# Layer 0 attention of a two-layer kernel: probability sums on GpSimd, value matmuls in two halves between the scores, three work banks

## The chip, the cores and the metric

The kernel runs on one core of a Trainium2 chip. The metric is the device time of one execution in microseconds. PE is TensorE (matmuls; PEld is its weight loads), ACT is ScalarE, DVE is VectorE, POOL is GpSimd, SP is the queue that issues DMAs. PSUM has eight banks of 128 partitions by 512 float32; GpSimd's instructions here read and write SBUF alone.

## The reference, cut to what matters

The program is two transformer layers with several kinds of attention and feed-forward. The change touches the first attention only: two batches of 1024 tokens, hidden size 128, 16 heads of 64, 4 key/value heads, causal.

```
q = (h @ Wq.T) ... ; k, v likewise with 4 heads, each repeated 4 times
scores = einsum("bhqd,bhkd->bhqk", q, k) * 64 ** -0.5 + causal
probs  = softmax(scores)          # exp(s - max) / sum over keys
out    = einsum("bhqk,bhkd->bhqd", probs, v) ... @ Wo.T
```

## The kernel before, in words

`stage_attention64` works in 8 **groups** g, one for each key/value head and batch; a group holds 4 query heads (`REP`). A group has 12 **steps**: a step is one tile of 128 keys (`kt`) against one **chunk** of 512 queries (`qc`). Chunk 0 has key tiles 0 to 3, chunk 1 has 0 to 7. Where a key tile lies on the diagonal the step is narrower: `unit_lo` leaves 512, 384, 256 or 128 query columns in the last four tiles of a chunk. So a group has 4,608 query columns, as many as nine full steps of 512.

In step n PE computes the scores of step n, transposed (keys on partitions): for each head one fp32r matmul with 128 rows (`qA`,`kH`, line 539) and a second of 65 rows (`qB`,`kL`, line 540) that adds the small parts and the negated row maximum. Three score banks take turns. ACT writes exp of them as float32 into a probability tile (line 723); three such tiles take turns (`P64`, `RING = 3`). On diagonal tiles GpSimd zeroes one 128-column block of each head by an affine select (line 740). Two steps later (`LAG = 2`), as the last thing of its step, PE runs `values(n)`: eight float32 matmuls (line 562; the trace shows two records for each) of 32 output columns each, that four at a time fill the four column strips of the array and add probabilities times V into the banks `O[0]` and `O[1]`; then four more of the same form with a matrix of ones (line 566) that add the row sums of the probabilities into a bank of their own, `SUMS`.

Between the scores PE does **jobs** for the next group ("fills"): `proj` (line 491, the q and k projections, split by ACT at lines 695 and 698 and by DVE at lines 606 and 611 into a high and a low part), `max` (lines 501 and 507, scores of raw form whose row maximum DVE takes, line 621), `turn` (line 513, a transpose of the maxima, which four DMAs lay into `qB`), and for a finished chunk `fin` (line 519, the output projection, which DVE adds to `y`, line 633). A job writes one of two work banks in turn, and PE waits until DVE has freed the bank of the job two before it. `spread_over` assigns `proj` and `max` jobs to steps by their column width, `proj` with weight 3; `parts` hands a step's jobs out after its score matmuls, ceil(jobs / score jobs) after each until none is left. The last group has no `proj` or `max` jobs to do.

When a chunk is closed, `copy_out` takes O[0] (ACT, line 707), the sums into `S64` (DVE, line 642) and O[1] (DVE, line 643) out of PSUM; SP gathers the sums into a dense tile (line 776), DVE takes reciprocals (line 649), SP writes them to DRAM and spreads them over partitions (lines 784, 789), DVE multiplies (line 656, both inputs in SBUF), and `fin` follows. After the last chunk DVE takes the reciprocal straight from `SUMS` (line 673), PE spreads it with a selection matrix (line 582). Each engine runs its own program in the written order, with semaphores between them.

## Time and profile before

| | us |
|---|---|
| three runs | 1538.16, 1543.96, 1883.71 |
| median | 1543.96 |
| the profiled execution, first to last instruction (span) | 1535.8 |
| layer 0 attention in it, first score matmul to last sum matmul | 60.4 to 662.5 |

A window or a timeline gives times from the span's start. "Busy" of PE is modelled, since matmuls are pipelined; what a matmul costs in a dense stream is read from the distance between two starts. In a row of the timeline, brackets give the engine's idle time before the instruction and what ended it.

### The profile page before, as it was taken

To read this page: it belongs to the slowest core of one execution; us is meant where nothing else is said; L and a number is where in the kernel's file an instruction comes from. 1 tells how busy PE (TensorE), PEld (TensorE's weight loads), DVE (VectorE), ACT (ScalarE), POOL (GpSimd) and SP (SyncE) were. 2 spreads that over 40 slices of the span, in tenths; PEclk is the share of its full clock that TensorE was granted. 3 is DMA by queue.
4 is the path that set the end of the run, shared out by engine and by line. 5 is a ranking of instruction groups with operands and counts; after the bars stand their busy time and mean duration, and the time that the engine had idled before them with its cause. 6 is when DMAs were issued, how large, how long until landed. Compare 5 with 4: busy or idle time off the path is not lost. (4 is left out here: it accounts for less than half of the span.)

```text
span 1535.8 us, 21410 instructions
## 1 busy us (share of the span) xinstructions
PE 1313.7 (86%) x7772; PEld 774.5 (50%) x7772; DVE 976.1 (64%) x1750; ACT 692.4 (45%) x1319; POOL 115.2 (7%) x155
## 2 busy tenths in 40 slices
PE   4688999999999999966999996526898888789998
PEld 3344444454545454444888874413343333256886
DVE  4455464545555454146999985756777666257998
ACT  2232334342424252433666665421566556525664
POOL 0000000000000000000000000120211111020000
PEclk9698999999999999987999998855899989868998
DMA  3101111120201020104576640022222210102220
GB/s 103 40 15 34 29 34 34 33 48 15 48 19 43 15 43 15 30 0 96 130 159 146 150 92 1 1 35 90 56 55 57 47 47 20 43 21 78 76 103 28
DMA packets 51476, 81.61 MB, mean 53 GB/s; under 512 B 16749, under 2 KB 34453, under 8 KB 47445
## 3 DMA queue, kind: packets, MB, share of 16 engines
q1 hardware_dynamic: 51004, 79.40, 21.1%
q10 hardware_dynamic: 384, 1.05, 0.6%
q8 instruction: 55, 0.90, 0.3%
q14 instruction: 33, 0.26, 0.1%
HBM read 63.75 MB, written 5.68 MB: 45 GB/s over the span
## 5 line engine op out<-in xcount | busy, mean ns | idle before, releaser
L621 DVE TENSOR_REDUCE mraw<-ps 128x1 f32<-128x512 f32 (+3 forms) x304 | 192.7, 659 | 131.1 <-PE ps L507 74.0
L1329 PE MATMUL ps<-qA 128*128 128x512 f32 x960 | 252.9, 400 | 15.2 <-POOL qA L1439 10.6
L723 ACT ACTIVATE shared<-ps 128x512 f32<-128x512 f32 (+1 forms) x216 | 119.4, 567 | 263.3 <-PE ps L540 261.9
L1046 DVE TENSOR_REDUCE mraw<-ps 128x2 f32<-128x1024 f32 (+3 forms) x160 | 173.7, 1114 | 67.6 <-PE ps L954 46.1
L1329 PEld LDWEIGHTS ps<-qA 128*128 128x128 f32 x960 | 182.1, 192 | 64.2 <-POOL qA L1439 12.3
L1101 ACT ACTIVATE shared<-ps 128x512 f32<-128x512 f32 (+2 forms) x320 | 154.4, 561 | 124.7 <-PE ps L970 124.4
L539 PE MATMUL ps<-qA,kH 128*128 128x512 f32 (+3 forms) x384 | 167.8, 447 | 5.8 <-DMA qB<-mT 5.8
L501 PE MATMUL ps<-kH,qA 128*128 128x512 f32 (+3 forms) x384 | 138.8, 415 | 34.9 <-DVE qA L611 18.8
L1393 ACT CAST qA<-shared 128x512 fp32r<-128x512 f32 x160 | 99.3, 621 | 90.4 <-DVE shared L1531 88.9
L1341 PE MATMUL ps<-qA,kH 128*128 128x512 f32 x480 | 136.3, 393 | 4.1 <-DVE qA L1455 4.1
L540 PE MATMUL ps<-qB,kL 65*128 65x512 f32 (+3 forms) x384 | 132.8, 356 | 0.0
L539 PEld LDWEIGHTS ps<-qA,kH 128*128 128x128 f32 x384 | 75.3, 196 | 80.1 <-issue 61.8
L1455 DVE TENSOR_TENSOR qA<-shared,qA 128x512 fp32r<-128x512 f32 x160 | 110.0, 688 | 7.0 <-ACT qA L1393 2.0
L501 PEld LDWEIGHTS ps<-kH,qA 128*128 128x128 f32 x384 | 70.2, 198 | 83.7 <-DVE mraw L621 52.6
L1531 DVE TENSOR_TENSOR shared<-shared 128x512 f32<-128x512 f32 x156 | 106.7, 684 | 0.0
L1341 PEld LDWEIGHTS ps<-qA,kH 128*128 128x128 f32 x480 | 90.1, 189 | 25.1 <-DVE qA L1455 6.4
L562 PE MATMUL ps<-shared 128*32 128x512 f32 (+3 forms) x1024 | 100.9, 512 | 0.3 <-DVE oU L643 0.3
L723 ACT ACTIVATE rB<-ps 128x512 f32<-128x512 f32 x88 | 51.8, 598 | 107.9 <-PE ps L540 107.0
L970 PE MATMUL ps<-qA,kH 64*128 64x512 f32 (+3 forms) x288 | 79.7, 443 | 14.5 <-ACT shared L1101 7.6
L943 PE MATMUL ps<-kL,qA 64*128 64x512 f32 (+3 forms) x288 | 67.3, 452 | 25.5 <-DMA kH<-qB 16.5
L611 DVE TENSOR_TENSOR qA<-ps,qA 64x512 fp32r<-64x512 f32 x64 | 44.1, 689 | 70.6 <-ACT qA L698 70.1
L996 PE MATMUL ps<-shared,VP 128*32 128x512 f32 (+3 forms) x768 | 87.3, 530 | 0.8 <-ACT oU L1088 0.5
(247 smaller groups left out, 1747.1 us busy)
## 6 DMA issues: line engine op xcount, KB each, us to landing
shared<-comb SPq DMA_DIRECT2D x92, 256.0 KB, 4.3
qB<-qA SPq DMA_DIRECT2D x16, 512.0 KB, 4.8
rB<-a0rec_dram SPq DMA_DIRECT2D x60, 128.0 KB, 2.9
shared<-comb SPq DMA_DIRECT2D x7, 1024.0 KB, 4.4
rB<-a1rec_dram SPq DMA_DIRECT2D x28, 128.0 KB, 2.6
e0wUp<-in_w SPq DMA_DIRECT2D x48, 64.0 KB, 4.6
qA<-q_split SPq DMA_DIRECT2D x24, 128.0 KB
q_split<-qA SPq DMA_DIRECT2D x4, 512.0 KB
```

Source lines behind the costliest of these rows:

```text
L501: ins = nc.tensor.matmul(bank[:, i * width:(i + 1) * width], k.qA[par][:, h0 + i, qt * P:(qt + 1) * P], k.kH[par][:, ch * 512:ch * 512 + w ...
L539: nc.tensor.matmul(out, k.kH[par][:, keys], k.qA[par][:, h, cols], start=True, stop=False)
L540: ins = nc.tensor.matmul(out, k.kL[par][0:hd + 1, keys], k.qB[par][0:hd + 1, h, cols], start=False, stop=True)
L562: nc.tensor.matmul(O[p][CT * at:CT * (at + 1), lo:512], v, probs(n)[:, 2 * p + i, lo:512], start=first, stop=last, skip_group_check=True)
L621: nc.vector.tensor_reduce(out[:, h0:h0 + n_h, qt % 4], src, AX, ALU.max).then_inc(w_free, 1)
L723: nc.scalar.activation(probs(n)[:, hs[0]:hs[-1] + 1, lo:512], src, ACT.Exp, scale=scale)\
L1046: nc.vector.tensor_reduce(out[:, :, js[0]:js[-1] + 1, qt % 4], src, AX, ALU.max).then_inc(x_free, 1)
L1101: nc.scalar.activation(dst, src, ACT.Exp, scale=scale).then_inc(p_done, 1)
L1329: ins = nc.tensor.matmul(bank[0:M, :], w[par][:, at:at + M], h[:, cols], start=(r == 0), stop=(r == 2))
L1341: ins = nc.tensor.matmul(acc(ch), w[par][:, m * D:(m + 1) * D], f[0:M, i % 2, :], start=(opens and r == 0), stop=(closing and r == 2), ski ...
L1455: nc.vector.tensor_tensor(fL[0:M, i % 2, :], k.hid[0:M, i % 2, :], fH[0:M, i % 2, :].bitcast(F32), ALU.subtract).then_inc(a_full, 1)
L1531: nc.vector.tensor_tensor(k.hid[0:M, i % 2, :], mul, rows, ALU.mult).then_inc(f_full, 1)
```

## The change

- **Sums.** The ones matmuls are gone from `values`, and `SUMS` with them. ACT writes the probabilities of a chunk's first key tile into an accumulator (`acc64`, one for each chunk, in memory that was `oN64` and `VP`) instead of a ring tile; GpSimd adds each later tile to it in place (float32, only the columns that the step has). A new job `sum` runs four ones matmuls over the accumulator once a chunk, into a work bank, and DVE copies that to `S64` (for the last chunk takes its reciprocal); SP gathers from there.
- **Order in a step.** `values` is two halves, one for each O bank. `woven_step` lays scores, halves and jobs evenly by their cost: a half stands behind the first half of the scores, the other behind the last, and jobs are spaced over all of them.
- **Work banks.** Three instead of two (0, 1 and 7).
- **New waits.** GpSimd's first add of a chunk waits until PE has read the first tile; ACT waits for GpSimd's add before it writes a ring tile again; PE's `sum` waits for the chunk's last add; an affine select stands behind the adds ahead of it in GpSimd's order.
- **Moved.** `sum` of chunk 0 in step 6, of chunk 1 in step 2 of the next group; reciprocals, multiplication and `fin` one step later than before; the multiplication works in place, `rB64` is one buffer for both chunks.

```diff
+    W_BANKS = (0, 1, 7)
+    NW = len(W_BANKS)
...
+    adds = [0]
...
+        adds.append(adds[-1] + (UNITS[n % NU][1] > 0))
+    ringed = [n for n in range(STEPS) if UNITS[n % NU][1] > 0]
...
-        plan.setdefault(NU * g + 10, []).append(("fin", g, 0, 0))
-        plan.setdefault(NU * (g + 1) + 6, []).append(("fin", g, 1, 0))
+        plan.setdefault(NU * g + 6, []).append(("sum", g, 0, 0))
+        plan.setdefault(NU * g + 11, []).append(("fin", g, 0, 0))
+        plan.setdefault(NU * (g + 1) + (2 if g + 1 < G else 1), []).append(("sum", g, 1, 0))
+        plan.setdefault(NU * (g + 1) + 7, []).append(("fin", g, 1, 0))
...
-    def parts(n):
-
-        heads = score_jobs(n) if n < STEPS else [()]
+    def woven_step(n):
+
+        main = []
+        if n < STEPS:
+            w = 512 - unit_lo(n)
+            jobs = score_jobs(n)
+            main += [((2 * i + 1) / (2 * len(jobs)), "score", i, 2 * w * len(hs)) for i, hs in enumerate(jobs)]
+        if n >= LAG:
+            w = 512 - unit_lo(n - LAG)
+            main += [((p + 1) / 2, "values", p, 4 * w) for p in range(2)]
         fills = due.get(n, [])
-        size = -(-len(fills) // len(heads))
-        return [(hs, fills[size * i:size * (i + 1)]) for i, hs in enumerate(heads)]
+        whole = sum(m[3] for m in main)
+        out, at, done = [], 0, 0
+        for _, kind, i, cost in sorted(main):
+            out.append((kind, i))
+            done += cost
+            while at < len(fills) and (2 * at + 1) * whole <= 2 * len(fills) * done:
+                out.append(("job", fills[at]))
+                at += 1
+        return out + [("job", idx) for idx in fills[at:]]
...
+        def work_bank(idx):
+            return k.bank(W_BANKS[idx % NW])
 
         def probs(n):
 
-            return k.P64[n % RING]
+            if UNITS[n % NU][1] == 0:
+                return k.acc64[chunk_of(n) % 2]
+            return k.P64[adds[n] % RING]
+
+        def chunk_of(n):
+            return 2 * (n // NU) + UNITS[n % NU][0]
+
+        def opening(c):
+            return NU * (c // 2) + 4 * (c % 2)
...
-                    bank = k.bank(idx % 2)
-                    if idx >= 2:
-                        pe.wait_ge(w_free, idx - 1)
+                    bank = work_bank(idx)
+                    if idx >= NW:
+                        pe.wait_ge(w_free, idx - NW + 1)
...
+                    elif kind == "sum":
+                        pe.wait_ge(summed, adds[opening(2 * g + qc + 1)])
+                        for h in range(REP):
+                            ins = nc.tensor.matmul(bank[CT * h:CT * (h + 1), :], k.ones[:, 0:CT],
+                                                   k.acc64[qc][:, h, :], start=True, stop=True,
+                                                   skip_group_check=True)
+                        ins.then_inc(w_full, 1)
...
-                def values(n):
+                def values(n, p):
...
-                    if on_diagonal(n):
+                    if p == 0 and on_diagonal(n):
                         pe.wait_ge(masked, diagonals[n + 1])
-                    else:
+                    elif p == 0:
                         pe.wait_ge(p_done, first_score[n + 1])
                     if kt == 0 and n:
-                        pe.wait_ge(o_act, 2 * g + qc)
-                        pe.wait_ge(o_dve, 2 * g + qc)
+                        pe.wait_ge((o_act, o_dve)[p], 2 * g + qc)
                     lo = unit_lo(n)
-                    first, last = kt == 0, closes(n)
-                    for p in range(2):
-                        for i in range(2):
-                            for half in range(2):
-                                at = 2 * i + half
-                                v = k.V[:, b * TPB + kt, kv * hd + half * CT:kv * hd + (half + 1) * CT]
-                                nc.tensor.matmul(O[p][CT * at:CT * (at + 1), lo:512], v,
-                                                 probs(n)[:, 2 * p + i, lo:512], start=first, stop=last,
-                                                 skip_group_check=True)
-                    for h in range(REP):
-                        ins = nc.tensor.matmul(SUMS[CT * h:CT * (h + 1), lo:512], k.ones[:, 0:CT],
-                                               probs(n)[:, h, lo:512], start=first, stop=last, skip_group_check=True)
+                    for i in range(2):
+                        for half in range(2):
+                            at = 2 * i + half
+                            v = k.V[:, b * TPB + kt, kv * hd + half * CT:kv * hd + (half + 1) * CT]
+                            ins = nc.tensor.matmul(O[p][CT * at:CT * (at + 1), lo:512], v,
+                                                   probs(n)[:, 2 * p + i, lo:512], start=(kt == 0), stop=closes(n),
+                                                   skip_group_check=True)
                     ins.then_inc(pv_done, 1)
...
-                    for at, (hs, fills) in enumerate(parts(n)):
-                        if hs:
-                            scores(n, first_score[n] + at, hs)
-                        for idx in fills:
-                            job(idx)
-                    if n >= LAG:
-                        values(n - LAG)
-                pe.wait_ge(o_dve, 2 * G)
+                    for kind, i in woven_step(n):
+                        if kind == "score":
+                            scores(n, first_score[n] + i, score_jobs(n)[i])
+                        elif kind == "values":
+                            values(n - LAG, i)
+                        else:
+                            job(i)
+                pe.wait_ge(w_free, index["sum", G - 1, 1, 0] + 1)
...
+                    elif kind == "sum":
+                        dve.wait_ge(w_full, idx + 1)
+                        if (g, qc) == (G - 1, 1):
+                            nc.vector.reciprocal(k.S64[:, :], bank).then_inc(w_free, 1)
+                        else:
+                            nc.vector.tensor_copy(k.S64[:, :], bank).then_inc(w_free, 1)
...
-                    dve.wait_ge(pv_done, n + 1)
+                    dve.wait_ge(pv_done, 2 * n + 2)
                     if g:
-                        dve.wait_ge(on_done, 2 * g + qc - 1)
-                    nc.vector.tensor_copy(k.S64[:, :], SUMS)
+                        dve.wait_ge(w_full, index["fin", g - 1, qc, 0] + 1)
                     nc.vector.tensor_copy(k.oU64[:, 1, cols], O[1]).then_inc(o_dve, 1)
...
-                    if at in (3, 5) and n >= NU:
-                        (recips if at == 3 else normalise)(n // NU - 1, 1)
-                    if at in (7, 9):
-                        (recips if at == 7 else normalise)(n // NU, 0)
+                    if at in (4, 6) and n >= NU:
+                        (recips if at == 4 else normalise)(n // NU - 1, 1)
+                    if at in (8, 10):
+                        (recips if at == 8 else normalise)(n // NU, 0)
...
-                    act.wait_ge(pv_done, n + 1)
+                    act.wait_ge(pv_done, 2 * n + 1)
                     if g:
-                        act.wait_ge(on_done, 2 * g + qc - 1)
+                        act.wait_ge(w_full, index["fin", g - 1, qc, 0] + 1)
                     nc.scalar.copy(k.oU64[:, 0, qc * 512:(qc + 1) * 512], O[0]).then_inc(o_act, 1)
+
+                def reuse(n):
+
+                    c = chunk_of(n)
+                    if UNITS[n % NU][1] == 0:
+                        if c >= 2:
+                            act.wait_ge(w_full, index["sum", c // 2 - 1, c % 2, 0] + 1)
+                    elif adds[n] >= RING:
+                        held = ringed[adds[n] - RING]
+                        act.wait_ge(pv_done, 2 * held + 2)
+                        act.wait_ge(summed, adds[held] + 1)
...
-                    if n >= RING and n < STEPS:
-                        act.wait_ge(pv_done, n - RING + 1)
-                    for at, (hs, fills) in enumerate(parts(n)):
-                        if hs:
+                    if n < STEPS:
+                        reuse(n)
...
+                    lo = unit_lo(n)
+                    pool.wait_ge(p_done, first_score[n + 1])
                     if on_diagonal(n):
-                        lo = unit_lo(n)
-                        pool.wait_ge(p_done, first_score[n + 1])
                         tile = probs(n)[:, :, lo:lo + P]
                         nc.gpsimd.affine_select(tile, tile, [[0, REP], [1, P]], ALU.is_ge, 0.0, base=0,
                                                 channel_multiplier=-1).then_inc(masked, 1)
+                        pool.wait_ge(masked, diagonals[n + 1])
+                    if adds[n + 1] > adds[n]:
+                        c = chunk_of(n)
+                        pool.wait_ge(pv_done, 2 * opening(c) + 2)
+                        if adds[n]:
+                            pool.wait_ge(summed, adds[n])
+                        total = k.acc64[c % 2][:, :, lo:512]
+                        nc.gpsimd.tensor_tensor(total, total, probs(n)[:, :, lo:512], ALU.add).then_inc(summed, 1)
...
-                    sp.wait_ge(o_dve, 2 * g + qc + 1)
+                def gather_sums(g, qc, idx):
+
+                    sp.wait_ge(w_free, idx + 1)
...
+                    if kind == "sum" and (g, qc) != (G - 1, 1):
+                        gather_sums(g, qc, idx)
...
+        k.acc64 = [k.oU[:, 2:4, :].rearrange("p a q -> p (a q)").rearrange("p (h q) -> p h q", h=REP),
+                   k.VP[:, :, :, :].rearrange("p t v e -> p (t v e)").rearrange("p (h q) -> p h q", h=REP)]
```

On PE, in the middle of the second chunk of the first group: one step of 512 columns, its jobs (`kH1`, `qA1`: next group) and the values of the step two before. Before:

```order
L501 MATMUL ps<-kH1,qA1 128x512 x2
L539 MATMUL ps<-qA0,kH0 128x512
L540 MATMUL ps<-qB0,kL0 128x512
L501 MATMUL ps<-kH1,qA1 128x384
L507 MATMUL ps<-masks,ident_bf 128x128
L501 MATMUL ps<-kH1,qA1 128x384
L507 MATMUL ps<-masks,ident_bf 128x128
L539 MATMUL ps<-qA0,kH0 128x512
L540 MATMUL ps<-qB0,kL0 128x512
L562 MATMUL ps<-shared 32x512 x8
L566 MATMUL ps<-shared,ones 32x512 x4
```

The same place of the changed program:

```order
L533 MATMUL ps<-kH1,qA1 128x512
L598 MATMUL ps<-shared 32x512 x4
L533 MATMUL ps<-kH1,qA1 128x512
L578 MATMUL ps<-qA0,kH0 128x512
L579 MATMUL ps<-qB0,kL0 128x512
L533 MATMUL ps<-kH1,qA1 128x512
L578 MATMUL ps<-qA0,kH0 128x512
L579 MATMUL ps<-qB0,kL0 128x512
L533 MATMUL ps<-kH1,qA1 128x384
L539 MATMUL ps<-masks,ident_bf 128x128
L598 MATMUL ps<-shared 32x512 x4
```

Two max jobs stood side by side between two scores and now stand apart; the values are in two pieces of four matmuls, each with other work on both sides; the ones matmuls are gone.

On POOL, from the first step of the stage on (`shared` and `rB` are ring tiles). Before:

```order
L740 AFFINE_SELECT shared<-shared 128x4x128 x2
L740 AFFINE_SELECT rB<-rB 128x4x128
L740 AFFINE_SELECT shared<-shared 128x4x128
L740 AFFINE_SELECT rB<-rB 128x4x128
L740 AFFINE_SELECT shared<-shared 128x4x128 x2
```

In the changed program (`oU` and `VP` are the accumulators of chunk 0 and chunk 1):

```order
L786 AFFINE_SELECT oU<-oU 128x4x128
L786 AFFINE_SELECT shared<-shared 128x4x128
L795 TENSOR_TENSOR oU<-oU,shared 128x4x384
L786 AFFINE_SELECT shared<-shared 128x4x128
L795 TENSOR_TENSOR oU<-oU,shared 128x4x256
L786 AFFINE_SELECT rB<-rB 128x4x128
L795 TENSOR_TENSOR oU<-oU,rB 128x4x128
L795 TENSOR_TENSOR VP<-VP,shared 128x2048 x2
L795 TENSOR_TENSOR VP<-VP,rB 128x2048
L786 AFFINE_SELECT shared<-shared 128x4x128
L795 TENSOR_TENSOR VP<-VP,shared 128x2048
```

An add now stands between two affine selects, and three full adds without a select open the second chunk.

On PE, the end of the stage. Before:

```order
L562 MATMUL ps<-shared 32x384 x8
L566 MATMUL ps<-shared,ones 32x384 x4
L562 MATMUL ps<-shared 32x256 x8
L566 MATMUL ps<-shared,ones 32x256 x4
L562 MATMUL ps<-rB,shared 32x128 x8
L566 MATMUL ps<-rB,ones 32x128 x4
L582 MATMUL ps<-S,sel 128x512 x2
```

In the changed program (`VP` is the accumulator of the last chunk):

```order
L598 MATMUL ps<-rB,shared 32x384 x4
L598 MATMUL ps<-shared 32x256 x8
L598 MATMUL ps<-shared 32x128 x4
L550 MATMUL ps<-VP,ones 32x512 x4
L598 MATMUL ps<-shared 32x128 x4
L615 MATMUL ps<-S,sel 128x512 x2
```

The one ones block over the accumulator stands ahead of the last half of the last values.

## Rows read from the trace of the kernel before

**Rows 1.** The page, the span.

```profile
span 1535.8 us, 21410 instructions
```

**Rows 2.** Windows: length, busy (count) PE PEld DVE ACT POOL, clock, DMA, GB/s.

```profile
60.30:166.00 105.70, 91.83 (x477) 46.32 (x478) 55.46 (x90) 30.88 (x54) 5.62 (x8) 0.88 0.11 25
314.80:388.10 73.30, 69.56 (x478) 35.16 (x477) 38.20 (x62) 28.24 (x50) 5.43 (x8) 1.00 0.13 33
388.10:462.90 74.80, 71.13 (x478) 36.04 (x477) 38.05 (x62) 28.24 (x50) 5.44 (x8) 0.98 0.14 34
611.80:662.20 50.40, 50.05 (x434) 25.23 (x437) 7.10 (x11) 20.51 (x40) 5.08 (x8) 1.00 0.08 23
```

**Rows 3.** Timeline of PE, last group: start us, length us, instruction, count.

```profile
643.45 0.40 PE L539 MATMUL ps<-qA,kH 128*128 128x512 f32 x1
643.68 0.40 PE L540 MATMUL ps<-qB,kL 65*128 65x512 f32 x1
...
644.22 0.39 PE L540 MATMUL ps<-qB,kL 65*128 65x512 f32 x1
644.54 1.92 PE L562 MATMUL ps<-shared 128*32 128x512 f32 x16
646.28 1.04 PE L566 MATMUL ps<-shared,ones 128*32 128x512 f32 x8
647.25 0.44 PE L539 MATMUL ps<-qA,kH 128*128 128x384 f32 x1
```

**Rows 4.** Waits, groups 2 to 5 (240.6 to 537.5): total us, times, longest.

```profile
PE ps L501 <- DVE qA L611: 7.7, 4, 1.9
PE ps L501 <- DVE mraw L621: 3.9, 14, 0.4
...
PEld ps L501 <- DVE mraw L621: 24.8, 61, 0.8
PEld ps L501 <- DVE qA L611: 9.4, 4, 2.4
...
DVE rs L649 <- DMA sm<-S: 11.4, 4, 3.5
```

**Rows 5.** Timeline of PE where group 2's fourth step ends.

```profile
258.14 1.02 PE L491 MATMUL ps<-hT,wqk 128*128 128x512 f32 x2
258.60 0.74 PE L501 MATMUL ps<-kH,qA 128*128 128x384 f32 x1
...
261.85 0.44 PE L501 MATMUL ps<-kH,qA 128*128 128x384 f32 x1 [1.91 <-DVE qA L611]
```

**Rows 6.** Windows, the 3.4 us after that wait.

```profile
263.30:266.70 3.40, 3.40 (x13) 1.41 (x15) 0.48 (x2) 2.00 (x4) 0.00 (x0) 0.50 0.02 5
```

**Rows 7.** Lines of POOL by form, whole kernel: count, busy us, mean ns.

```profile
L740 POOL TENSOR_SCALAR_AFFINE_SELECT shared<-shared 128x512 f32<-128x512 f32 x40 | 25.4, 634 | 252.5 <-ACT shared L723 252.5
...
L1439 POOL TENSOR_TENSOR qA<-e1wUp,qA 128x512 fp32r<-128x512 f32 x1 | 1.3, 1270 | 43.0 <-ACT qA L1383 43.0
L1439 POOL TENSOR_TENSOR kH<-e1wD,kH 128x256 fp32r<-128x256 f32 x1 | 0.7, 733 | 0.0
```

**Rows 8.** Timeline of POOL, then of DVE, in group 6.

```profile
591.88 0.99 POOL L740 TENSOR_SCALAR_AFFINE_SELECT rB<-rB 128x512 f32<-128x512 f32 x1 [38.43 <-ACT rB L723]
...
602.65 0.63 POOL L740 TENSOR_SCALAR_AFFINE_SELECT shared<-shared 128x512 f32<-128x512 f32 x1 [3.96 <-ACT shared L723]
...
591.16 1.22 DVE L656 TENSOR_TENSOR oU<-oU,rB 128x1024 f32<-128x1024 f32 x1
...
601.13 2.05 DVE L621 TENSOR_REDUCE mraw<-ps 128x1 f32<-128x512 f32 x3 [3.28 <-PE ps L501]
```

**Rows 9.** Lines, attention stage (46 to 668): DVE's maxima.

```profile
L621 DVE TENSOR_REDUCE mraw<-ps 128x1 f32<-128x512 f32 (+3 forms) x304 | 192.7, 659 | 131.1 <-PE ps L507 74.0 <-PE ps L501 51.4
```

**Rows 10.** Timeline, last chunk: third step's end, and the last reciprocal.

```profile
637.54 0.50 PE L539 MATMUL ps<-qA,kH 128*128 128x512 f32 x1
...
662.57 3.36 DVE L673 RECIPROCAL S<-ps 128x512 f32<-128x512 f32 x1 [7.59 <-PE ps L566]
```

More of the change, by code:

```diff
@@ L600, in take @@
                     par, b = g % 2, g % B
-                    bank = k.bank(idx % 2)
+                    bank = work_bank(idx)
                     if kind == "proj":
@@ L688, in high @@
                     par = g % 2
-                    bank = k.bank(idx % 2)
+                    bank = work_bank(idx)
                     if qc == 0 and j == 0 and g >= 2:
@@ L714, in _ @@
                         copy_out(n - LAG - 1)
[L715 to L718 removed]
+                    if n < STEPS:
+                        reuse(n)
+                    for kind, i in woven_step(n):
+                        if kind == "score":
                             lo = unit_lo(n)
[L720 removed]
+                            s, hs = first_score[n] + i, score_jobs(n)[i]
                             act.wait_ge(s_full, s + 1)
@@ L724, in _ @@
                                 .then_inc(p_done, 1)
-                        for idx in fills:
-                            if JOBS[idx][0] == "proj":
-                                high(idx)
-                act.wait_ge(pv_done, STEPS)
-                act.wait_ge(on_done, 2 * G - 2)
+                        elif kind == "job" and JOBS[i][0] == "proj":
+                            high(i)
+                act.wait_ge(pv_done, 2 * STEPS)
+                act.wait_ge(w_full, index["fin", G - 2, 1, 0] + 1)
                 nc.scalar.copy(k.oU64[:, 0, 512:1024], O[0])
```

29 lines of the change are left out of this document (12 added, 17 removed).

## The prediction

> **What bounds the kernel now.** Only layer 0's attention changes, some 602 of the span's 1535.8 us [rows 1], so I cut it into groups, from a group's first exp to the next group's [rows 2]. Groups 1 to 6 take 73.3 to 74.8 us each, group 0 105.7, group 7, which has no projections and maxima to do, 50.4. In a middle group PE is busy 69.6 of 73.3 us, DVE 38.2, ACT 28.2, POOL 5.4: PE is the only engine that can be the bound. But PE's busy time is modelled, so I next read what its work costs from distances between starts [rows 3]: a score matmul of 512 columns follows the one before by 0.23 us, the sixteen records of one step's values take 1.74, and the eight of its sums 0.97 until the next score starts. The values' rate gives 0.87 for the sums; the other 0.10 is the switch from 32-column work back to a full array. The way in costs 0.32 - 0.23 = 0.09 (643.45 to 643.68 against 644.22 to 644.54). One visit to 32-column work thus costs 0.19 us beside its matmuls.
>
> The waits come next [rows 4]. In groups 2 to 5, `max` matmuls (L501) wait for DVE: 7.7 + 3.9 us in which PE had drained, and 24.8 + 9.4 us of weight loads, of which a part lies under the matmul before. [Rows 5] show the longest sort: a projection starts at 258.14, the next job takes the other work bank, and the one after that needs the projection's bank, which ACT and DVE must read first. It starts at 261.85, after 1.91 us of drained PE. Of the 65 weight-load waits I count all but 0.2 us each (the reader sees 0.41 us a time where matmuls are 0.23 apart): 34.2 - 13 = 21 us in four groups, **5.3 us a group**; the ends are 11.6 / 4 = 2.9 and 34.2 / 4 = 8.5. Behind that wait the clock is granted at 0.50 for 3.4 us [rows 6], that is 1.2 instead of 2.4 GHz: some 1.7 us of work lost. Group 3, whose clock is 1.00, is 1 to 1.5 us shorter than its neighbours.
>
> **The change on PE, a middle group.** A group has 4,608 columns, nine full steps.
> 1. Sums removed: 9 x 0.87 = -7.8 us. Their switches stay, since the values have them too.
> 2. Two `sum` jobs: each 0.87 + 0.19, together +2.1.
> 3. The values in two visits: in ten of twelve steps other work stands between the halves, 10 x 0.19 = +1.9 (none if a switch hides behind a job: 0; all twelve: 2.3).
> Together -3.8 us, which is less than the removed matmuls suggest.
> 4. Order and third bank. A job now stands behind each score or so: two score matmuls and the job's own, 3 x 0.23 = 0.69 us from the next at the closest, and 0.97 more where a half of the values lies between. DVE's maximum takes 0.66 [rows 9], and a job waits for the third before it, not the second: 261.85 - 258.14 = 3.7 us is then about the time in which PE gets there anyway. I take back 4.5 of the 5.3 us (ends 2 and 6, and 1.4 more if the slow clock goes too).
> 5. ACT and DVE copy an O bank just before the half that overwrites it; ACT's copy may still run when the first half is due in the narrow third step. +0.3 us (ends 0 and 1, which also holds a late select, below).
> A middle group: -3.8 - 4.5 + 0.3 = **-8.0**, six of them **-48 us**.
>
> **The change on the other engines.** GpSimd gets eleven adds a group, and the trace of this stage has none. The nearest rows are three adds in the expert stage [rows 7]: 0.73 us for 256 elements a partition, 1.27 for 512, so 2.1 ns an element, and 1.27 + 1536 x 0.0021 = 4.5 us for a full step of 2,048 (3.4, 2.35 and 1.27 for the narrower ones). In a group four full adds and two of each narrower size: 18 + 14.1 = 32.1 us, with eight selects of 0.63 **37.2 us**, beside a PE that needs 73.3 or 74.8 less 8.0, say 66. That is hidden as long as no deadline is missed. The tightest: the first add of chunk 0 waits until PE has read the first tile, at the end of the third step; the third step's select stands behind it, 3.4 + 0.63 + waits = 4.2 us later. PE has the fourth step to do (values of 384 columns 1.74 x 0.75 + 0.19 = 1.5, scores of 128 columns at least a quarter of 8 x 0.23 = 0.5, one or two jobs 0.3 to 1.7) and then two full scores (0.93) before it wants that tile: 3.2 to 4.6 us. So the select is between on time and 1 us late, the end named in item 5. In chunk 1 the ring tile of the first add is wanted a full step later, 66 / 9 = 7.3 us against 4.5. DVE loses nothing: the copy of the sums only changes its place. Its reciprocal still waits some 2.9 us for the gather [rows 4], now with three banks to cover it. SP's gather moves behind the `sum` job, and `fin` a step later; nobody waits for `fin` but `copy_out` a group later.
>
> **Group 0** has the same work at a mean clock of 0.88 [rows 2]: 3.8 / 0.88 = 4.3, and the same 4.5 of waits: **-9** (ends -4 and -13).
>
> **Group 7** has no jobs between, so here POOL is the slower one. From the end of the last chunk's third step its order takes 3 x 4.5 + 5.1 + 4.05 + 2.98 + 1.9 = 27.6 us, and then the sum 1.1: 28.7. Before, PE took from there (637.54) to the reciprocal (662.57) 25.0 [rows 10]: +3.7. The steps ahead of it save 4.25 x 0.87 = 3.7 of sums and 1.7 of a `fin` that moves out, and pay 2.1 + 0.9 for two `sum` jobs and switches: -2.4. Together **+1.5** (ends -3.8 and +6).
>
> **Sum.** -48 - 9 + 1.5 = -55.5 us on 1535.8. The three runs' median stands 8.2 above that span and their lowest 2.4; I add 6: **1486 us**.
>
> **A page against this change.** In [rows 8] a select of GpSimd takes 0.99 us instead of 0.63 when it meets DVE's multiplication, whose two inputs lie in SBUF, and 0.63 in the middle of DVE's maxima, which read PSUM. By the rows, then, only two multiplications a group (2 x 1.2 us) stretch the adds. The Trainium skill, GPSIMD Engine Reference, section "Key points", says that GpSimd shares its SBUF interfaces with VectorE and contends with instructions of a two-port mode or with two SBUF inputs, and its section "Engine selection" sends elementwise adds to VectorE; by its rule on two inputs, the trace agrees.
>
> **Rivals.**
> - *POOL becomes the bound.* If adds stop for every DVE instruction and not for the multiplication alone, 37.2 us of POOL work beside 38.2 of 73.3 us of DVE stretch to 37.2 / (1 - 0.52) = 78 us a group, and ACT's ring wait holds PE to that, 4 us above today's 74. It decides where POOL's work reaches PE's 66, at 1.77 times its price: a full add of 8 us instead of 4.5. Six groups +4 each, group 0 +3, group 7 +8: 1535.8 + 35 + 6 = 1577. Against it: the 0.63 beside the maxima; for it: no add of 2,048 was ever seen here. Chance 0.07, **slower**.
> - *The waits stay.* The waits for DVE come from the chain projection, cast, subtraction, maximum, not from the banks: then only 2 us of item 4 come back, the switches cost 2.3 and item 5 its 1: -7.8 + 2.1 + 2.3 - 2 + 1 = -4.4 a group; 6 x -4.4 - 4 + 6 = -24, so 1535.8 - 24 + 6 = 1518. For it: DVE's subtraction of [rows 5] needs ACT's cast first, which stands between exps. Chance 0.20, **within 2%** for the most part.
> - *All waits go, the slow clock too.* -3.8 - 6 - 1.4 = -11.2 a group: -67 - 13 - 4 = -84, so 1458. Chance 0.13.
>
> **Chances.** The forecast holds 0.60, its own range 1465 to 1505. About 2% can be told from no change, that is 31 us of 1543.96: below 1513, above 1575. Faster: 0.60 + 0.13 + 0.01 of the second rival, 0.74; within: 0.19; slower: 0.07. The range leaves out the first rival and the outer ends of the other two: 1456 to 1527.
>
> **What would show it.** A middle group of about 66 us from first exp to first exp (the maximum of the claim is 62, its failure 70 or more). PE's L501 waits (its new line) on DVE well under 2 us a group. GpSimd's full add near 4.5 us, its busy time near 37 us a group, and no row in which PE's values or ACT's exps wait for POOL, except in group 7, where both should. From the start of a half of a full step to the next score 0.97 us. Wrong would be: full adds of 6 us or more; exps that wait for POOL in groups 1 to 6; a longer half-speed stretch in the last chunk.

## The result and the profile after

The changed kernel takes **1468.79 us** in the median of four runs. The kernel before takes 1538.16 beside it in the median of three, a fourth and slow run of 1883.71 us being left out. The ratio is 0.9544, 95% interval 0.9517 to 0.9571, some 4.6% faster. The forecast was 1486 with a range of 1456 to 1527. The profiled execution took 1468.17, its span is 1466.5. The span is 69.3 us shorter than that of before [rows 1].

The windows below cut the changed kernel into groups as before, from a group's first exp to the next group's (group 7 up to the last reciprocal). A row has the length, then busy time and count of PE, PEld, DVE, ACT and POOL, then clock, DMA share and GB/s.

```profile
59.60:155.30 95.70, 80.65 (x403) 41.80 (x403) 62.00 (x90) 30.44 (x54) 37.79 (x18) 0.89 0.12 27
...
283.90:348.10 64.20, 64.05 (x397) 31.99 (x397) 40.17 (x63) 27.66 (x50) 38.13 (x18) 1.00 0.16 37
...
540.90:596.00 55.10, 49.53 (x351) 21.78 (x349) 10.02 (x12) 21.05 (x40) 38.19 (x18) 0.97 0.07 20
```

The six middle groups (first exps at 155.3 and 540.9) take 64.3 us each; before, their mean was 74.3 ((611.8 - 166.0) / 6, [rows 2]). PE is now busy 64.05 of 64.20 us in the one shown, and the clock is 1.00 in every one. GpSimd's 5.4 us became 38.1. Where the 69.3 us came from:

| stretch | before | after | difference | predicted |
|---|---|---|---|---|
| up to the first exp of group 0 | 61.6 | 59.6 | -2.0 | 0 |
| group 0 (from its first exp; the window of [rows 2] begins 1.3 earlier, with the first scores) | 104.4 | 95.7 | -8.7 | -9 |
| groups 1 to 6 | 445.8 | 385.6 | -60.2 | -48 |
| group 7, to the last reciprocal | 50.8 | 55.2 | +4.4 | +1.5 |
| the rest of the program | 873.2 | 870.4 | -2.8 | 0 |

The first and the last row are not shown to come from the change: over all kernels of this document the first stretch takes 58.4 to 61.6 us and the last 870 to 879, with the same code in the last.

The waits of groups 2 to 5 (total us, times, longest; compare [rows 4]), changed kernel:

```profile
POOL VP L795 <- PE ps L598: 47.9, 4, 12.0
...
PEld ps L533 <- DVE mraw L654: 26.0, 32, 0.8
...
PEld ps L533 <- DVE qA L644: 4.0, 8, 0.6
```

The two rows of [rows 4] in which PE had drained, 7.7 and 3.9 us, have no successor. (A row of PE is a drained wait: no matmul was running. A row of PEld is a weight load that waits, and it can lie under a running matmul.) In all six middle groups no row names POOL as what PE, ACT or DVE waits for; it is GpSimd that waits, 12 us a group, for PE to read a chunk's first tile. The weight loads still stand 26.0 us for DVE, and the timeline below shows why that costs nothing now. It has PE and PEld of the changed kernel, with the start, the length and the idle time before.

```profile
323.80 1.06 PE L598 MATMUL ps<-shared 128*32 128x512 f32 x8
324.80 0.30 PEld L533 LDWEIGHTS ps<-kH,qA 128*128 128x128 f32 x2 [0.84 <-DVE mraw L654]
324.80 0.50 PE L533 MATMUL ps<-kH,qA 128*128 128x256 f32 x2
```

The load stands still for 0.84 us while the half of the values (L598) runs on the array; the next matmul starts 1.00 us after the half's start, and 0.97 was foreseen as the spacing with no wait at all. The middle groups have 64 such places, a half of a full step and a max job behind it, and the spacing is 0.99 to 1.00 in all of them, whether the load waited or not.

The next lines, by form, are GpSimd's adds and selects and two of DVE's operations in the attention of the changed kernel (count, busy us, mean ns, idle before and what ended it).

```profile
L795 POOL TENSOR_TENSOR VP<-VP,shared 128x2048 f32<-128x2048 f32 x22 | 100.4, 4562 | 80.8 <-PE ps L598 54.2 <-ACT shared L770 24.4 <-POOL VP L795 1.7
L786 POOL TENSOR_SCALAR_AFFINE_SELECT shared<-shared 128x512 f32<-128x512 f32 x38 | 28.2, 742 | 32.6 <-ACT shared L770 32.6
...
L695 DVE TENSOR_TENSOR oU<-oU,rB 128x1024 f32<-128x1024 f32 x15 | 37.9, 2527 | 7.0 <-DMA rB<-a0rec_dram 7.0
...
L625 DVE COPY mmax<-mraw 128x16 f32<-128x16 f32 x7 | 5.0, 712 | 0.2
```

A full add takes 4.56 us. It is DVE's multiplication that got longer, from 1.22 us in [rows 8] to 2.53 in the mean.

In group 7 PE does wait for GpSimd: once for a select in chunk 0 (0.68 us), and at the end for selects (L786) three times, then for the last add. These are the drained waits of PE at the end:

```profile
581.14 1.06 PE L598 MATMUL ps<-shared 128*32 128x512 f32 x8 [1.24 <-POOL shared L786]
...
586.36 1.26 PE L598 MATMUL ps<-rB,shared 128*32 128x384 f32 x8 [1.42 <-POOL rB L786]
...
593.50 0.43 PE L598 MATMUL ps<-shared 128*32 128x128 f32 x8 [1.08 <-POOL shared L786]
594.94 1.06 PE L550 MATMUL ps<-VP,ones 128*32 128x512 f32 x8 [1.01 <-POOL VP L795]
```

### The profile page after: what moved, and what is told of

It is laid out like the page before. It is cut to its first block and busy times, and to the rows that moved or that the text cites. A ratio compares the mean times of both kernels' runs of the same rounds, so it can differ in the third digit from the quotient of the medians.

```text
span 1466.5 us, 20332 instructions
## 1 busy us (share of the span) xinstructions
PE 1262.6 (86%) x7132; PEld 746.9 (51%) x7132; DVE 997.7 (68%) x1750; ACT 689.9 (47%) x1319; POOL 376.7 (26%) x235
## 5 line engine op out<-in xcount | busy, mean ns | idle before, releaser
L654 DVE TENSOR_REDUCE mraw<-ps 128x1 f32<-128x512 f32 (+3 forms) x304 | 189.1, 656 | 71.0 <-PE ps L539 44.2
L578 PE MATMUL ps<-qA,kH 128*128 128x512 f32 (+3 forms) x384 | 161.6, 431 | 7.9 <-DMA qB<-mT 7.9
L770 ACT ACTIVATE shared<-ps 128x512 f32<-128x512 f32 (+1 forms) x163 | 89.4, 567 | 148.6 <-PE ps L579 144.3
L795 POOL TENSOR_TENSOR VP<-VP,shared 128x2048 f32<-128x2048 f32 (+3 forms) x38 | 137.2, 3609 | 82.2 <-PE ps L598 54.2
L1448 ACT CAST qA<-shared 128x512 fp32r<-128x512 f32 x160 | 99.3, 621 | 91.3 <-DVE shared L1586 90.9
L533 PE MATMUL ps<-kH,qA 128*128 128x512 f32 (+3 forms) x384 | 133.0, 396 | 9.0 <-DVE qA L644 6.7
L533 PEld LDWEIGHTS ps<-kH,qA 128*128 128x128 f32 x384 | 69.2, 196 | 103.1 <-DVE mraw L654 50.5
L1177 POOL TENSOR_SCALAR_AFFINE_SELECT shared<-shared 128x512 f32<-128x512 f32 x64 | 40.6, 635 | 277.9 <-ACT shared L1156 277.9
L598 PE MATMUL ps<-shared 128*32 128x512 f32 (+3 forms) x864 | 88.5, 484 | 2.3 <-POOL shared L786 2.3
```

The source lines that it names most:

```text
L533: ins = nc.tensor.matmul(bank[:, i * width:(i + 1) * width], k.qA[par][:, h0 + i, qt * P:(qt + 1) * P], k.kH[par][:, ch * 512:ch * 512 + w ...
L578: nc.tensor.matmul(out, k.kH[par][:, keys], k.qA[par][:, h, cols], start=True, stop=False)
L654: nc.vector.tensor_reduce(out[:, h0:h0 + n_h, qt % 4], src, AX, ALU.max).then_inc(w_free, 1)
L795: nc.gpsimd.tensor_tensor(total, total, probs(n)[:, :, lo:512], ALU.add).then_inc(summed, 1)
L1448: nc.scalar.copy(fH[0:M, i % 2, :], k.hid[0:M, i % 2, :]).then_inc(f_high, 1)
```

## Experiments

The forecast's theory: a middle group gains by fewer matmuls on PE (items 1 and 2), pays for two visits (item 3), and wins most of its waits for DVE back by the order and the third bank together (item 4); GpSimd is hidden until its sum of work passes PE's. Rivals: the waits come from the chain and not from the banks, so that item 4 is worth little; and GpSimd decides earlier, by a single deadline. The kernel before took 1537.51 us beside the experiments up to "One visit", 1538.08 beside the next four that ran (the order alone, the dearer adds, the tail), and 1537.55 beside the two with the select first. Middle groups are compared by the mean of groups 2 to 5 where no other is named.

### The third bank

```diff
-    W_BANKS = (0, 1, 7)
+    W_BANKS = (0, 1)
```

> The changed kernel with two work banks (0 and 1) instead of three; all else as changed. Theory A (the even order alone takes the waits for a work bank away; the third bank is spare): 1468 to 1473 us, a middle group stays at 64 to 65 us. Theory B (the third bank takes them away): the waits come back, 3 to 5 us a group in seven groups, 1490 to 1505 us, and PE's max matmuls show drained idle time before them again.

1522.86 us, ratio to the kernel before 0.9894 (0.9861 to 0.9926). The rows are windows of two middle groups, and then the drained waits of groups 2 to 5, with two banks.

```profile
311.30:383.30 72.00, 67.47 (x398) 32.87 (x397) 41.16 (x63) 27.69 (x50) 38.14 (x18) 0.95 0.14 33
...
455.40:524.40 69.00, 64.42 (x397) 31.81 (x397) 41.34 (x63) 27.65 (x50) 38.18 (x18) 1.00 0.14 32
```

```profile
PE ps L533 <- DVE qA L644: 11.5, 8, 1.5
...
PE ps L533 <- DVE mraw L654: 6.2, 8, 1.3
```

The drained waits are back, 17.7 us in four groups against 11.6 in [rows 4], and with them the clock falls to 0.95 in three of these groups; the fourth keeps 1.00 and takes 69.0. The mean is 71.2 us against 64.3. In this order 54 of the change's 69 us hang on the bank (41 in the old order, below). Bank 7 was `SUMS` before: without the sums' move to GpSimd there is no third bank to have.

### The sums alone, then with the third bank

Both put the old order back: scores, after each its share of the jobs, both halves of the values at the step's end. The first also has two banks. The new `sum` jobs and GpSimd's adds stay.

```diff
...
+        size = -(-len(fills) // len(heads))
+        for at, i in enumerate(heads):
+            if i is not None:
+                out.append(("score", i))
+            out += [("job", idx) for idx in fills[size * at:size * (at + 1)]]
+        return out + [("values", p) for p in range(2) if n >= LAG]
```

> Only the sums moved: GpSimd adds, PE sums once a chunk; order in a step and two banks as before. If PE is the bound: 7.8 - 2.1 = 5.7 us a group in seven groups, nothing in the last: 1541 - 40 = 1501 us. If the freed PE time turns into waits for DVE on two banks: 1520 us or more, with longer waits of the max matmuls.

> Sums on GpSimd and three banks, but within a step the order of before: after each score a clump of jobs, both halves of the values together at the step's end. Theory A (order): the waits of before stay, but the extra switches (1.9 us a group) go: 1485 to 1500 us. Theory B (bank): the waits are gone anyway and the switches saved too: 1453 to 1462 us.

Sums alone: 1510.32 us, 0.9823 (0.9793 to 0.9853). With three banks and the old order: 1469.47, 0.9553 (0.9522 to 0.9583), not to be told from the change itself in the total. Its parts differ, though: a middle group is 0.7 us longer than the change's, group 0 takes 90.4 us against 95.7, group 7 54.2 against 55.1, and the program behind the last reciprocal 879.3 against 870.4. The rows are a window of a middle group and the waits of groups 2 to 5, sums alone.

```profile
370.40:439.90 69.50, 65.23 (x397) 32.98 (x397) 38.85 (x62) 28.15 (x51) 38.22 (x18) 0.98 0.14 37
```

```profile
PEld ps L524 <- DVE mraw L645: 25.2, 60, 1.3
PEld ps L524 <- DVE qA L635: 9.9, 6, 2.4
PE ps L524 <- DVE qA L635: 7.7, 4, 1.9
PE ps L524 <- DVE mraw L645: 5.3, 12, 0.8
```

The same, old order with three banks:

```profile
279.50:344.50 65.00, 62.41 (x397) 32.84 (x397) 40.72 (x62) 28.12 (x50) 38.22 (x19) 0.97 0.15 37
```

```profile
PEld ps L524 <- DVE mraw L645: 10.1, 20, 1.0
PEld ps L524 <- DVE qA L635: 7.3, 4, 1.8
PE ps L524 <- DVE qA L635: 6.7, 4, 1.7
...
PE ps L524 <- DVE mraw L645: 3.6, 8, 0.6
```

A group goes from 74.3 to 69.4 by the sums and to 65.0 by the bank. In the old order the weight loads' waits for DVE fall from 25.2 + 9.9 to 10.1 + 7.3 us in four groups, 4.4 us a group, and a group falls by 4.4. The drained waits fall by 0.7 of that, and the clock is no better. So the reading of [rows 4] that most of a weight load's wait counts agrees with this pair. What a third bank can't help is the projection's chain (6.7 us drained, 4 times), and one stretch of 3.4 us at half the clock is left in each group: the mean is 0.97. Against sums alone, the two-bank kernel with the even order and two visits takes 1.8 us a group more (71.2 to 69.4); the two visits have a price of 1.6 by the next run.

### One visit

The values of a step stand in one piece at the end of the even order.

```diff
-            main += [((p + 1) / 2, "values", p, 4 * w) for p in range(2)]
+            main += [(1.0, "values", 0, 8 * w)]
...
-            out.append((kind, i))
+            out += [(kind, p) for p in range(2)] if kind == "values" else [(kind, i)]
```

> The changed kernel with both halves of the values together at the end of the step, jobs still spread evenly over the step's work. By the price of a switch (0.19 us, ten a group): 1.9 us a group less, 62.4 us, 1455 us in all. Rival (the values in two pieces give DVE time between the jobs): waits for work banks come back, 1469 to 1480 us.

1458.55 us, 0.9491 (0.9461 to 0.952). The window of a middle group, one visit:

```profile
338.60:401.20 62.60, 61.54 (x397) 32.80 (x397) 40.24 (x63) 27.14 (x50) 38.27 (x18) 1.00 0.16 41
```

A group takes 62.65 us in the mean, 1.6 less than with two visits; ten switches of 0.19 us make 1.9. A little of the rival is there too: PE stands drained for a work bank for 3.7 us in four groups, where the change has none. The even order is worth keeping in the middle groups (the clock is 1.00 against 0.97 in the old order), the split is not.

### The order alone

The kernel before, sums on PE, two banks, with the even order and the split.

```diff
...
+            main += [((p + 1) / 2, "values", p, (4 + 4 * p) * w) for p in range(2)]
...
+                    if p == 0 and kt == 0 and n:
                         pe.wait_ge(o_act, 2 * g + qc)
                         pe.wait_ge(o_dve, 2 * g + qc)
```

> The kernel before with the merged order alone: sums stay on PE, two work banks, values in two visits (the second one does the sums). Theory A (the even order pays by itself, as a fill's wait is split into smaller ones): a middle group goes from 74.3 to about 72, 1525-1532 us. Theory B (with two banks an even order costs, as it did on the changed kernel, where two banks with the even order stood at about 71.7 us a group against 69.4 with the old order): +2 a group by the merging and visits, 76 to 77 us a group, 1550-1560 us.

1569.2 us, 1.0214 (1.0155 to 1.0273): slower, by more than either theory said. Windows of two middle groups:

```profile
244.60:321.60 77.00, 71.23 (x478) 34.19 (x476) 38.68 (x63) 27.80 (x51) 5.10 (x8) 1.00 0.14 33
321.60:402.60 81.00, 75.97 (x478) 36.11 (x476) 38.65 (x63) 27.79 (x51) 5.10 (x8) 0.94 0.13 30
```

Even at a clock of 1.00 a group takes 77.0, 3.7 us more than the group of before at 1.00 (73.30 in [rows 2]). PE is busy 1.7 us more in it (71.23 to 69.56), near the price of ten more visits. And it stands drained for 2.3 us for DVE's copy of an O bank (1.57) and an exp (0.7), which it does not in that group of before: in this kernel the first half waits for the copies of both O banks, in the change for its own alone. So the loss lies in the split and in that wait; a cost of the even spacing itself is not shown. The even order in one visit with two banks was not run.

### Dearer adds

Ahead of each add GpSimd makes one or two spare adds over half as many elements, into memory that nobody reads.

```diff
+                        nc.gpsimd.tensor_tensor(k.rB[:, S:S + 2 * (512 - lo)].rearrange("p (h q) -> p h q", h=2),
+                                                probs(n)[:, 0:2, lo:512], probs(n)[:, 0:2, lo:512], ALU.add)
                         nc.gpsimd.tensor_tensor(total, total, probs(n)[:, :, lo:512], ALU.add).then_inc(summed, 1)
```

> The changed kernel, and before each add on GpSimd a spare add of half its size, whose result nobody reads: a full add then costs 4.56 + 2.37 = 6.93 us, 1.52 times as much, and GpSimd's work in a middle group comes to about 55 us of 64.3. Theory A (the prediction's: GpSimd decides only when its sum passes the group, at 1.77 times the price): middle groups stay within 0.5 us of 64.3, only group 7, where GpSimd was already late, grows by 8 to 14 us: 1475-1485 us. Rival B (the deadlines decide earlier than the sum: a select behind a longer add delays the values, a ring of three tiles holds up the exponentials): middle groups grow by 2 us or more, 1490 us or more.

> As the run with the half-size spare add, but two of them, so that every add costs about twice: GpSimd's work in a middle group comes to about 72 us. Theory A: GpSimd becomes the bound there and a middle group takes 72 to 76 us, group 7 about 20 us more: 1545-1580 us, slower than before. Rival (GpSimd's lateness is caught up in other stretches): a middle group below 70 us, under 1525 us.

One spare add: 1511.82 us, 0.9818 (0.9775 to 0.9861). Two: 1584.79, 1.0302 (1.0261 to 1.0342), slower than before. The rows are the window of a middle group with one spare add, and the place in it where PE loses its time (rows of POOL, then of DVE, then of PE).

```profile
290.40:358.50 68.10, 65.64 (x397) 32.38 (x396) 41.26 (x63) 27.63 (x50) 51.45 (x29) 0.97 0.14 35
```

```profile
344.27 1.89 POOL L795 TENSOR_TENSOR rB<-shared 128x1024 f32<-128x1024 f32 x1
346.12 5.52 POOL L797 TENSOR_TENSOR VP<-VP,shared 128x2048 f32<-128x2048 f32 x1
351.60 0.63 POOL L786 TENSOR_SCALAR_AFFINE_SELECT shared<-shared 128x512 f32<-128x512 f32 x1
...
345.11 2.14 DVE L695 TENSOR_TENSOR oU<-oU,rB 128x1024 f32<-128x1024 f32 x1
...
352.28 0.85 PE L598 MATMUL ps<-shared 128*32 128x384 f32 x8 [2.33 <-POOL shared L786]
```

A spare half add takes 1.89 us, not 2.37, so with the 4.56 of the plain one a full add costs 6.45 here, 1.41 times as much (4.74 + 1.92 in the mean of this run, where some wait for DVE: 1.46 times). GpSimd works 51.45 of 68.1 us and is far from full. Yet a group is 3.9 us longer: the select of chunk 1's sixth tile (the expectation of the run below calls it the fifth) is issued behind an add that ends at 351.6, PE stands drained for 2.33 us, and behind it the clock is granted at 0.50 for 3.4 us. The rival was right, and the forecast's threshold of 1.77 wrong. Group 7, where GpSimd was late already, takes 73.6 us instead of 55.1. The next rows are the window of a group with two spare adds, and the waits of two groups.

```profile
311.90:389.30 77.40, 67.25 (x398) 33.17 (x399) 43.55 (x64) 27.64 (x50) 65.26 (x39) 0.93 0.12 31
```

```profile
ACT shared L770 <- POOL VP L800: 17.2, 4, 6.2
...
PE ps L598 <- POOL shared L786: 15.4, 4, 5.9
```

Here exps stand still for adds (the ring of three tiles) and values for selects. The rival "GpSimd becomes the bound" has the time about right (1577), but not by the sum of its work: 65.3 of 77.4 us are busy.

### The select ahead of the add

If one late select is the cost, it can be taken away: GpSimd selects the next tile before it adds this one. The adds of the kernel with one spare add are unchanged.

```diff
...
+                for n in range(STEPS):
...
+                    if n == 0:
+                        select(n)
+                    if n + 1 < STEPS:
+                        select(n + 1)
+                    if on_diagonal(n):
                         pool.wait_ge(masked, diagonals[n + 1])
```

> The kernel with the half-size spare adds (middle groups 68.2 us, of which GpSimd works 51.5), and on GpSimd the select of the next tile stands ahead of the add of this one. In that kernel's trace TensorE stands still 2.33 us a group for one select, the fifth tile's of the second chunk, that waits behind an add of 5.52 us, and half a window of slow clock follows. Theory A (that one late select is what the longer adds cost): middle groups come back to 64.3-65.5 us, 1483-1495 us. Rival B (the sum of GpSimd's work and the ring of three tiles set the pace; the exponentials are held up to 3.9 us for a tile that is not yet added): middle groups stay at 67.5 us or more, 1505 us or more.

1479.8 us, 0.9624 (0.9581 to 0.9667). The window of a middle group:

```profile
275.10:339.20 64.10, 63.96 (x398) 31.93 (x397) 39.01 (x63) 27.70 (x50) 51.39 (x29) 1.00 0.16 37
```

The same 51.4 us of GpSimd work, and the group is back at 64.1, at a clock of 1.00. So in the middle groups the order of GpSimd's own instructions set the time with dearer adds, not the amount of its work. The exps do wait for adds there, 7.6 us a group (15.2 in the two groups of 275.1 to 403.4), and it costs nothing. In group 7 the amount still counts: it takes 70.5 us. The total is below the expected range because group 0 gained too (87.9 us from first exp to first exp, against 94.8 with the select behind).

### The end of group 7

On top of the one-visit kernel, the last three tiles of the last chunk are not added by GpSimd; the last `sum` job runs their ones matmuls on PE.

```diff
...
+                        for n in late:
+                            lo = unit_lo(n)
+                            for h in range(REP):
+                                ins = nc.tensor.matmul(bank[CT * h:CT * (h + 1), lo:512], k.ones[:, 0:CT],
+                                                       probs(n)[:, h, lo:512], start=False, stop=(n == late[-1]),
+                                                       skip_group_check=True)
...
-                    if adds[n + 1] > adds[n]:
+                    if adds[n + 1] > adds[n] and n < STEPS - 3:
```

> The changed kernel with both halves of the values in one visit, and in the very last chunk the last three (narrow) tiles are not added by GpSimd; TensorE sums them in the final sum by 12 more short products. Theory A (the end of group 7 waits for GpSimd's backlog, whose last three adds take 3.44 + 2.36 + 1.26 us): about 5 us off the one-visit kernel's 1458.6, 1452-1455 us. Rival B (the exponentials or the values set the end): within 1.5 us of 1458.6.

1457.12 us, 0.9471 (0.9434 to 0.9507). By the intervals it is not to be told from the one-visit kernel; by the traces group 7 goes from 52.8 to 50.2 us, half of what was expected. The rows are PE and DVE at its end, with the tail on PE.

```profile
568.99 1.50 PE L605 MATMUL ps<-rB,shared 128*32 128x384 f32 x16 [2.23 <-POOL rB L793]
570.42 1.98 PE L565 MATMUL ps<-oU,woG 128*128 128x512 f32 x4
572.34 1.51 PE L605 MATMUL ps<-shared 128*32 128x256 f32 x32
573.66 1.04 PE L551 MATMUL ps<-VP,ones 128*32 128x512 f32 x8
...
576.06 3.36 DVE L673 RECIPROCAL S<-ps 128x512 f32<-128x512 f32 x1 [2.93 <-PE ps L557]
```

Behind the late select PE now has 7 us of its own work (values, `fin`, sums) in a row. The select itself still waits for the add ahead of it. So both were put together, tail on PE and select first:

> The kernel with one visit and the last three tiles summed by TensorE (1457.1 us, middle groups 62.6, group 7 50.2 to the start of the reciprocal), with the select ahead of the add as well. Theory A (group 7 waits for selects behind adds: 1.33 and 2.23 us at the fifth and sixth tile of its last chunk): group 7 2-3 us shorter, 1454-1455.5 us, middle groups unchanged. Rival B (in group 7 it is the backlog of adds, which the ring passes on to the exponentials; an add that waits for the next tile's exponential comes later still): group 7 the same or longer, 1457-1460 us.

**1441.96 us**, 0.9376 (0.934 to 0.9411), the fastest of all: 27 us below the change. The windows of a middle group and of group 7:

```profile
271.40:333.60 62.20, 61.52 (x398) 32.91 (x397) 39.44 (x63) 27.18 (x51) 38.20 (x19) 1.00 0.16 38
...
520.10:567.20 47.10, 46.46 (x375) 22.82 (x373) 9.84 (x13) 21.18 (x42) 33.81 (x17) 1.00 0.08 24
```

Group 7 is 3.1 us shorter, as theory A had it, and now below the kernel before's 50.8. The rest had not been expected: group 0 goes from 91.6 to 88.0 us, the middle groups from 62.65 to 62.2, and the program behind the last reciprocal, whose code is the same, from 877.6 to 873.6. That last stretch takes between 870 and 879 us in the profiles of these kernels; why is open.

## Why the prediction was right, and where not

**What bounds the kernel.** Right: PE, and more so after the change (64.05 of 64.20 us).

**Items 1 and 2, sums.** -5.7 us a group foreseen (-7.8 + 2.1), -4.9 measured (74.3 to 69.4). Near enough; the drained waits grew by 0.4 us a group (11.6 in [rows 4] to 13.0), and the rest of the gap was not traced.

**Item 3, two visits.** +1.9 foreseen, +1.6 measured (62.65 to 64.27). The price of a switch to 32-column work, which had been worked out from four distances in [rows 3], about holds.

**Item 4, order and third bank.** The step that was too small: -4.5 foreseen, -6.8 measured, near the lower end of its bounds (-6 and -1.4 more for the slow clock). The runs part it. The third bank alone is worth 4.4 (69.4 to 65.0). The rest, 2.4, is the even order (65.0 to 62.65 in one visit): the half-speed stretch of 3.4 us goes, 1.7 us of lost work by [rows 6], and the drained waits fall from 2.6 to 0.9 us a group. How much of the 2.4 belongs to either is not shown. All items together, -4.9 + 1.6 - 4.4 - 2.4, make the -10.0 a group but for rounding, where -8.0 had been forecast; six groups make the 12 us by which that term was missed. The rival "the waits stay" falls: in the change's order all drained waits hung on the bank (17.7 us in four groups with two banks, none with three). But the chain that it named kept its wait with three banks in the old order (6.7 us drained in four groups), and lost it by the even order. The rival "all waits go, the slow clock too" was the nearer one for the middle groups (-10.0 against its -11.2), and its total of 1458 is nearer to the 1468.8 than the forecast's 1486. Taking back 4.5 of 5.3 us of weight-load waits was right in size for the bank; leaving the slow clock out was a choice, and the wrong one.

**Item 5.** No wait for an O bank's copy and no late select shows in a middle group; the 0.3 us are within the rounding of the others.

**GpSimd.** 4.5 us a full add foreseen, 4.56 measured; 37.2 us a group, 38.1 measured. Three rows of 256 and 512 elements in another stage were enough to price an add of 2,048. But the threshold did not follow from it. The rival "POOL becomes the bound" was given its point at 8 us a full add, where the sum of work reaches PE's; at 6.45 us a group already lost 3.9. The prediction had named the right deadline in kind, a select behind an add, and then dropped it when it worked out the point.

**Group 0.** -9 foreseen, -8.7 measured, and that is luck. The runs part it: 104.4 us before, 99.3 by the sums alone, 90.4 with the third bank in the old order, 91.8 with the even order in one visit, 95.7 with the change. So the bank gave 8.9 here, and the even order and the split took 5.3 back; -4.3 for PE's work and -4.5 for waits had been foreseen.

**Group 7.** +1.5 foreseen, +4.4 measured, inside its ends. The prediction's GpSimd order begins at the first add of the last chunk, here at 565.49. From there to the reciprocal at 596.06 it takes 30.6 us instead of 28.7: one of the selects took 1.63 us instead of 0.63, behind DVE's multiplication (see the last section), and there are gaps of 0.17 us between adds. The steps ahead of that saved 1.1 us (25.7 to 24.6) instead of 2.4. The clock is 0.97 there, where it was 1.00 [rows 2]: from 586.66 it is granted at 0.50 for 3.4 us, behind the waits for GpSimd. The two terms of the forecast, +3.7 and -2.4, make 1.3 and not the 1.5 that went into its sum.

**The sum.** -55.5 foreseen on the span, -69.3 measured: 12.2 in the middle groups, 2.0 ahead of the first exp and 2.8 behind the last reciprocal, less 2.9 in group 7 and 0.3 in group 0. The 6 us added for the way from span to median were too many: the median stands 2.3 above the span. Together they are the 17 us between 1486 and 1468.8.

**What would show it.** Middle group 66: it is 64.3. No drained L501 wait (L533 now): so, though weight loads still wait. GpSimd's add and busy time: so. No values or exps that wait for GpSimd but in group 7: so. A half to the next score 0.97: 0.99 to 1.00, to a max job; in the middle groups no score stands directly behind a half of a full step. Of the signs of being wrong one came: a half-speed stretch in the last chunk, where before had none.

## What to carry to other kernels

A bank that a removed operation frees may be worth as much as the operation (4.4 and 4.9 us a group here), and an order that spaces work evenly was worth 2.4 us a group once the bank was there; with two banks it was run only together with the split into two visits, and the two made the kernel slower. Work that is moved to an idle engine is hidden as long as its deadlines hold, and a sum that fits is not enough; the short instruction that others wait for belongs ahead of the long one that nobody waits for. Group the work of one array shape, since every switch has a price (about 0.19 us a visit here).

## What the hardware showed that had not been expected

GpSimd's instructions on the one side, and DVE's multiplication and its copy within SBUF on the other, did not slow each other by a share; one waited for the other's end. The rows are DVE, then POOL, in the timeline of the changed kernel.

```profile
312.87 1.21 DVE L695 TENSOR_TENSOR oU<-oU,rB 128x1024 f32<-128x1024 f32 x1
...
327.79 0.24 DVE L687 RECIPROCAL rs<-sm 128x16 f32<-128x16 f32 x1
...
338.64 3.72 DVE L695 TENSOR_TENSOR oU<-oU,rB 128x1024 f32<-128x1024 f32 x1
...
326.99 4.58 POOL L795 TENSOR_TENSOR VP<-VP,rB 128x2048 f32<-128x2048 f32 x1 [0.17 <-POOL VP L795]
...
337.80 3.47 POOL L795 TENSOR_TENSOR VP<-VP,shared 128x1536 f32<-128x1536 f32 x1
341.44 1.41 POOL L786 TENSOR_SCALAR_AFFINE_SELECT rB<-rB 128x512 f32<-128x512 f32 x1 [0.17 <-ACT rB L770]
```

At 312.87, with GpSimd idle, the multiplication takes 1.21 us. At 338.64 an add is under way that ends at 341.27; 1.09 us later, at 342.36, the multiplication is done. All eight multiplications of the stage that begin inside an add end 1.08 to 1.09 us behind it; the seven others take 1.21 to 1.23. The select that was issued at 341.44 ends at 342.85, 0.49 us after that. In [rows 8] it is the same sum: multiplication until 592.38, select until 592.87. And where the multiplication was queued ahead of a full add, in the kernel with the spare add, the add took 5.52 us and ended 4.39 us after the multiplication, whose end is 347.25. DVE's copy of 16 elements (L625), 0.17 us alone, took 3.93 us in the one case in which it began inside an add, and ended with it. Not every DVE instruction within SBUF waits: the reciprocal (L687), with one input and its output in SBUF, takes 0.24 us at 327.79, in the middle of an add that ends at 331.56, and 0.24 to 0.25 us in all 14 cases that begin inside an add. DVE's maxima and additions that read PSUM kept their 0.69 us.

The prediction read [rows 8] as a stretching by overlap. The Trainium skill, SBUF — State Buffer, section "SBUF: two separate sides", says it outright: the port pair that the two engines share is an exclusive lock, whoever starts first holds it for the whole instruction, and the other is blocked; it names DVE operations with two SBUF inputs or in a two-port mode. By that rule, the traces agree, in both directions. The rival's 78 us a group, for which the adds had to stop for every DVE instruction, could not come about: a full add kept 4.56 us in the mean beside 40 us of DVE's work a group.

Nobody was waiting for the multiplication in the middle groups, so its 3.72 us cost nothing there. In group 7 the late select behind it cost about 1 us.
